# A state-space image block in float32: one norm stage's elementwise work spread over three engines, and an output stage that asks for its weights behind its first loads

## The chip, the cores and the metric

The kernel runs on one core of a Trainium2 chip. The core has five engines that the profile names: PE (matrix multiply, with its weight loads shown as PEld), DVE (vector), ACT (activation functions), POOL (general purpose) and SP, which here only issues DMAs. They run their own instruction streams and meet through semaphores. The metric is device time in microseconds (us) of one execution. All data is float32.

## The reference, cut to what matters

The input is an image `x` of 1024 channels by 64 x 64 pixels. Two blocks are computed, each added to its input:

```
x = x + conv(ln_c(x))            # ln_c: normalised over channels, at each pixel
t = tokens(x)                    # 4096 tokens (pixels) of 1024 channels
t = t + ffn(ln_t(t))             # ln_t: normalised over channels, at each token

conv(v):                         # a recurrence along the 1024 channels, for every pixel
    n  = layernorm2d(v) * w + b          # mean and variance over the 4096 pixels of a channel
    dt = softplus(n . dt_w + dt_b)       # n . dt_w sums over one image row of 64 pixels
    h[c] = exp(-exp(log_A) * dt[c]) * h[c-1] + n[c]      # out = h, for each pixel
ffn(v):
    x, z  = split(v @ in_proj)           # 2048 columns each
    y     = selective_scan(conv1d(x)) + the same backwards    # 16 states for each of 2048 columns
    out   = nan_to_num((y * silu(z)) @ out_proj)
```

The reference writes the recurrence of `conv` as a masked matrix of cumulative sums; it is the same function.

## The kernel before, in words

The program is six stages, one behind the other, each a block in which every engine has a written-out instruction list; a barrier stands between stages. Nothing is scheduled by a planner: the order on each engine is the order in the code, and loops (`Fori`) run on the engines with register addresses. A `wait_ge` holds an engine until a semaphore has reached a count; `then_inc` raises it when the instruction is done.

**Stages.** Channel norm, pixel variance, channel scan (`stage_channel_scan`, tensors `n_...` and `norm_...` in the trace), token norm, the large selective scan (`stage_scan`), and the output product (`stage_out`). The change touches the third and the last.

**Channel scan.** `xn`, the normalised input, stays in SBUF whole: 32 tiles of 128 pixels by 1024 channels. The loop takes two tiles (`s` = 0, 1) at a time, 16 pairs `j`. For a pair:

- POOL multiplies the tile by `rstd2` (L297, `scaled`). In the kernel before POOL waits for nothing here and goes through all 32 tiles at once, in place.
- DVE applies the affine part `* lnw + lnb`, in place (L315, `affine`, `normed`).
- PE sums image rows with the weights `dt_w` (L406, into PSUM `dt_ps`), and transposes the original input (L415, into PSUM `xt`).
- Softplus is `max(v, 0) + ln(1 + exp(-|v|))`: DVE does the maximum (L323, `relu`, reads PSUM), ACT does `Abs`, `Exp`, `Ln` (L384, L387, L390), DVE adds the two (L330, `add_log`, both inputs in SBUF).
- ACT forms the decay `exp(a * softplus)` (L395).
- DVE runs the recurrence (L336, `scan`: inputs `decay` and `xn`, both in SBUF), adds the transposed input (L341, one input in PSUM), takes statistics (L346, L350) and copies two numbers per tile (L353).

DVE's order inside the loop is `affine(j+1)`, `relu(j)`, `scan(j-1)`, `add_log(j)`. `relu(j)` waits for the decay of pair `j-1`, since both use the tile `softplus`.

**Output stage.** The 4096 tokens are 8 chunks of 512. For each chunk, 16 units of 128 columns are prepared: three loads of 256 KB (`yf`, `yb`, `z`), POOL adds `yb` to `yf` (L1278), ACT takes `silu(z)` (L1287), PE transposes the sum (L1299), DVE multiplies into `yg` (L1327). Then 8 projections follow (`project`, L1309): each is 16 matmuls of 512 columns that read all 16 units of `yg` and one eighth of the weights `wout` (1 MB), and DVE cleans, adds the residual and SP stores. `chunks` sets the order on every engine: chunk 0 is prepared whole, and from then on each step prepares one pair of units of the next chunk and then projects one eighth of this one. So PE transposes 18 units, the 16 of chunk 0 and the first pair of chunk 1, ahead of its first projection. SP runs one pair further ahead (`ahead=1`). The loads go into two buffers (`s`), reused when DVE has multiplied the unit (`gated`); the eight 1 MB loads of `wout` are asked for one at a time, one behind each pair of units of chunk 0 (L1256), and PE's first projection waits for all eight.

Of the kernel before, what the change touches and what calls it, by code (L numbers as in the profile page):

```python
# [260 lines left out]
def stage_channel_scan(nc, passed, xn, ident, rstd2, mv, x_d, lnw_d, lnb_d, dtw_d, dtb_d, loga_d):  # L261
    with Scope(nc, "n3") as sc:
# [30 lines left out]
        @block.gpsimd  # L293
        def _(pool):

            with pool.Fori(0, NT) as t:
                nc.gpsimd.tensor_tensor(xn[:, ds(t * C, C)], xn[:, ds(t * C, C)], rstd2[:],  # L297
                                        ALU.mult).then_inc(scaled, 1)

        @block.vector  # L300
        def _(dve):
# [10 lines left out]
            def affine(j):  # L312
                for s in range(2):
                    dve.wait_ge(scaled, j * 2 + s + 1)
                    nc.vector.tensor_scalar(xn[:, ds(j * (2 * C) + s * C, C)], xn[:, ds(j * (2 * C) + s * C, C)],  # L315
                                            lnw[:, ds(j * 2 + s, 1)], lnb[:, ds(j * 2 + s, 1)],
                                            ALU.mult, ALU.add).then_inc(normed, 1)

# [6 lines left out]

            def add_log(j):
                for s in range(2):
                    dve.wait_ge(log_done, j * 2 + s + 1)
                    dve.wait_ge(relu_done, j * 2 + s + 1)
                    nc.vector.tensor_tensor(sp_[:, s], sp_[:, s], mag[:, s], ALU.add).then_inc(sp_done, 1)  # L330
# [33 lines left out]
            affine(0)  # L364
            step(0, before=False)
            with dve.Fori(0, NT // 2 - 2) as i:
                step(i + 1)
            step(NT // 2 - 1, after=False)
# [3 lines left out]
        def _(act):  # L372
            act.wait_ge(par_loaded, 5 * LOAD)
            nc.scalar.activation(aneg[:], aneg[:], ACT.Exp).then_inc(achain, 1)
            act.wait_ge(achain, 1)
            nc.scalar.mul(aneg[:], aneg[:], -1.0).then_inc(achain, 1)
            act.wait_ge(achain, 2)
            act.sem_inc(decay_done, 2)
            act.sem_inc(scan_done, 2)
            with act.Fori(0, NT // 2) as j:  # L380
# [7 lines left out]
                for s in range(2):  # L388
                    act.wait_ge(ab_done, j * 4 + s + 3)
                    nc.scalar.activation(mag[:, s], mag[:, s], ACT.Ln, bias=1.0).then_inc(log_done, 1)  # L390
                for s in range(2):
                    act.wait_ge(par_loaded, 5 * LOAD)
                    act.wait_ge(sp_done, j * 2 + s + 1)
                    act.wait_ge(scan_done, j * 2 + s + 1)
                    nc.scalar.activation(decay[:, s], sp_[:, s], ACT.Exp,  # L395
                                         scale=aneg[:, ds(j * 2 + s, 1)]).then_inc(decay_done, 1)

# [800 lines left out]
def stage_out(nc, passed, ident, yf_d, yb_d, z_d, wout_d, x1T_d, out_d):  # L1198
    with Scope(nc, "out") as sc:
        wout = sc.sb("wout", [P, KT, DB, P])  # L1200
        yg = sc.sb("yg", [P, 2, DB, T])
        yf, yb = sc.sb("yf", [P, 2, T]), sc.sb("yb", [P, 2, T])
        z, sz = sc.sb("z", [P, 2, T]), sc.sb("sz", [P, 2, T])
# [4 lines left out]
        w_loaded, const_ready = sc.sem("w_loaded"), sc.sem("const_ready")  # L1208
        y_loaded, x_loaded = [sc.sem(f"y_loaded{s}") for s in range(2)], [sc.sem(f"x_loaded{s}") for s in range(2)]
# [7 lines left out]


# [23 lines left out]
        def _(sp):  # L1242
# [3 lines left out]
            def prepare(c, g, q):  # L1246
                for s in range(2):
                    db = 2 * q + s
                    hold(sp, gated, c * DB + db + 1, passed)
                    sp.dma_start(yf[:, s], yf_d[ds(c * DB + db + 1, 1)].rearrange("o p t d -> (o p) (t d)")  # L1250
                                 ).then_inc(y_loaded[s], LOAD)
                    sp.dma_start(yb[:, s], yb_d[ds((NCH - 1) * DB + db + 1 - c * DB, 1)]  # L1252
                                 .rearrange("o p t d -> (o p) (t d)")).then_inc(y_loaded[s], LOAD)
                    sp.dma_start(z[:, s], z_d[db * P:(db + 1) * P, ds(c * T, T)]).then_inc(y_loaded[s], LOAD)  # L1254
                if isinstance(c, int) and c == 0:
                    sp.dma_start(wout[:, q], wout_d[q]).then_inc(w_loaded, LOAD)  # L1256
# [13 lines left out]
        def _(pool):  # L1270
# [4 lines left out]
            def prepare(c, g, q):  # L1275
                for s in range(2):
                    pool.wait_ge(y_loaded[s], c * (KT * 3 * LOAD) + (q + 1) * 3 * LOAD)
                    nc.gpsimd.tensor_tensor(yf[:, s], yf[:, s], yb[:, s], ALU.add).then_inc(summed, 1)  # L1278
# [4 lines left out]
        def _(act):  # L1283
            def prepare(c, g, q):
                for s in range(2):
                    act.wait_ge(y_loaded[s], c * (KT * 3 * LOAD) + (q + 1) * 3 * LOAD)
                    nc.scalar.activation(sz[:, s], z[:, s], ACT.Silu).then_inc(silu_done, 1)  # L1287
# [4 lines left out]
        def _(pe):  # L1292
            def prepare(c, g, q):
                for s in range(2):
                    u = 2 * q + s
                    pe.wait_ge(summed, c * DB + u + 1)
                    pe.wait_ge(gated, c * DB + u + 1)
                    for tb in range(TB):
                        last = nc.tensor.matmul(yt_ps[:, s, tb * P:(tb + 1) * P], yf[:, s, tb * P:(tb + 1) * P],  # L1299
# [125 lines left out]
```

## Time and profile before

| | us |
|---|---|
| median of 3 runs | 8618.31 (8612.55 to 8621.57) |
| the profiled execution's own time | 8615.87 |
| its span, first to last instruction | 8614.1 |
| channel scan, 189.3 to 499.1 of the span | 309.8 |
| output stage, 7561.0 to 8614.1 | 1053.1 |
| of it, until the first projection starts at 7641.96 | 81.0 |

A row of the trace's timeline reads: start, duration, engine, line, operation, output <- inputs, shape, count; consecutive instructions of one line are merged, and the bracket says how long the engine sat idle before it and what ended that. A duration of merged instructions goes from the first start to the last end. A row of "windows" has the stretch and its length, then for PE, PEld, DVE, ACT and POOL the busy time and the number of instructions, then the granted clock of PE as a share of its full speed, the mean busy share of the 16 DMA engines and the rate in GB/s. A row of "waits" has who waited, for whom, us in total, times and the longest.

### The profile page before, as it was taken

What the parts mean: (1) busy time and instruction counts of PE and PEld (TensorE: products, weight loads), DVE (VectorE), ACT (ScalarE), POOL (GpSimd) and SP (SyncE); (2) the same over time, 40 slices, a digit from 0 to 9 for tenths busy, and PEclk for the clock granted to TensorE, in tenths of its full rate; (3) what the DMA queues carried; (4) which work ended last, traced back from release to release, by engine and by line L of the source; (5) the groups of instructions that cost most, each with busy time, mean ns of one, the idle gap of its engine ahead of it and who ended that gap; (6) DMA issues with size and microseconds to landing.
All of it is one profiled execution on the core that took longest, in us unless ns stands there. A gap on an engine that the chain in (4) does not pass through costs nothing. (4 is left out here: it accounts for less than half of the span.)

```text
span 8614.1 us, 107712 instructions
## 1 busy us (share of the span) xinstructions
PE 7207.2 (84%) x28624; PEld 4128.4 (48%) x28624; DVE 7548.3 (88%) x8364; ACT 4928.4 (57%) x11720; POOL 6814.0 (79%) x3026
## 2 busy tenths in 40 slices
PE   7449888888888888876788888888888887769999
PEld 4243455455545555544455545455555555534444
DVE  7940999999999999999999999999999999934443
ACT  2552666666666666666666666666666666610000
POOL 1310999999999999999999999999999999921110
PEclk9679999999999999987899999999999998879999
DMA  3263231313131313121223232323232322154442
GB/s 83 58 188 129 73 112 64 113 65 114 64 113 67 113 64 113 66 100 42 98 73 124 74 126 72 124 76 124 72 124 78 122 73 104 47 175 137 137 138 81
DMA packets 540787, 843.35 MB, mean 98 GB/s; under 512 B 112576, under 2 KB 260032, under 8 KB 522816
## 3 DMA queue, kind: packets, MB, share of 16 engines
q1 hardware_dynamic: 540224, 837.03, 29.4%
q8 instruction: 208, 3.41, 0.2%
q14 instruction: 355, 2.91, 0.1%
HBM read 583.83 MB, written 253.02 MB: 97 GB/s over the span
## 5 line engine op out<-in xcount | busy, mean ns | idle before, releaser
L1114 POOL TENSOR_TENSOR scan_w<-scan_du,scan_bcast_b 128x2048 f32<-128x2048 f32 x1023 | 4629.4, 4537 | 3.6 <-DMA scan_bcast_b<-bc 3.6
L1163 DVE TENSOR_TENSOR_SCAN scan_h<-scan_da,scan_state,scan_w 128x512 f32<-128x512 f32 x3072 | 3787.0, 1282 | 21.8 <-issue 14.5
L920 PE MATMUL scan_yT<-all_ident,scan_hc 128*128 128x128 f32 x12288 | 1992.4, 300 | 1010.9 <-DVE scan_hc L1173 995.5
L1020 ACT ACTIVATE scan_da<-scan_delta,scan_prm 128x512 f32<-128x512 f32 x4096 | 2803.6, 685 | 0.0
L920 PEld LDWEIGHTS scan_yT<-all_ident,scan_hc 128*128 128x128 f32 x12288 | 1466.6, 151 | 1974.6 <-DVE scan_hc L1173 1741.8
L1173 DVE TENSOR_TENSOR scan_hc<-scan_h,scan_bcast_c 128x512 f32<-128x512 f32 x3072 | 1955.5, 682 | 16.9 <-ACT scan_state L1000 16.9
L812 PE MATMUL scan_in_ps<-scan_hn,scan_win 128*128 128x512 f32 x3840 | 1741.0, 596 | 13.3 <-issue 13.3
L1000 ACT ACTIVATE scan_state<-scan_h 128x1 f32<-128x1 f32 x3072 | 518.6, 169 | 1770.7 <-DVE scan_h L1163 1768.8
L1123 POOL TENSOR_TENSOR scan_hp<-scan_hs,scan_bcast_c 128x512 f32<-128x512 f32 x1024 | 1306.5, 1276 | 73.7 <-issue 47.0
L1163 DVE TENSOR_TENSOR_SCAN scan_hs<-scan_da,scan_state,scan_w 128x512 f32<-128x512 f32 x1024 | 1297.5, 1267 | 32.1 <-ACT scan_da L1020 31.9
L812 PEld LDWEIGHTS scan_in_ps<-scan_hn,scan_win 128*128 128x128 f32 x3840 | 697.0, 192 | 723.2 <-issue 723.2
L1309 PE MATMUL out_o_ps<-out_yg,out_wout 128*128 128x512 f32 x2048 | 891.5, 594 | 0.0
L819 PE MATMUL scan_dt_ps<-scan_x,scan_diag 128*128 128x512 f32 x1920 | 882.3, 602 | 0.0
L1278 POOL TENSOR_TENSOR out_yf<-out_yf,out_yb 128x512 f32<-128x512 f32 x128 | 163.8, 1279 | 753.6 <-DMA out_z<-z 753.6
L887 PE MATMUL scan_yT<-all_ident,scan_hp 128*128 128x128 f32 x4096 | 714.3, 304 | 0.0
L1309 PEld LDWEIGHTS out_o_ps<-out_yg,out_wout 128*128 128x128 f32 x2048 | 386.1, 191 | 465.2 <-issue 465.2
L887 PEld LDWEIGHTS scan_yT<-all_ident,scan_hp 128*128 128x128 f32 x4096 | 562.4, 158 | 0.0
L1287 ACT ACTIVATE out_sz<-out_z 128x512 f32<-128x512 f32 x128 | 80.7, 630 | 836.2 <-DMA out_z<-z 836.2
L819 PEld LDWEIGHTS scan_dt_ps<-scan_x,scan_diag 128*128 128x128 f32 x1920 | 353.5, 194 | 356.9 <-issue 356.9
L1338 DVE COPY out_o<-out_o_ps 128x512 f32<-128x512 f32 x64 | 44.3, 692 | 523.4 <-PE out_o_ps L1309 316.5
L1000 ACT ACTIVATE scan_state<-scan_hs 128x1 f32<-128x1 f32 x1024 | 205.4, 201 | 318.2 <-DVE scan_hs L1163 317.1
L824 PE MATMUL scan_proj_ps<-scan_xc_out,scan_wx 128*96 128x512 f32 x512 | 384.1, 843 | 0.2
(128 smaller groups left out, 5547.8 us busy)
## 6 DMA issues: line engine op xcount, KB each, us to landing
yT<-scan_y_out SPq DMA_DIRECT2D x257, 256.0 KB, 2.0
scan_win<-winx SPq DMA_DIRECT2D x128, 512.0 KB, 3.5
xc<-scan_xc_out SPq DMA_DIRECT2D x256, 256.0 KB, 2.0
scan_xc<-xc SPq DMA_DIRECT2D x256, 256.0 KB, 3.6
scan_bcast_b<-bc SPq DMA_DIRECT2D x64, 1024.0 KB, 7.8
scan_bcast_c<-bc SPq DMA_DIRECT2D x64, 1024.0 KB, 7.8
scan_win<-winz SPq DMA_DIRECT2D x128, 512.0 KB, 4.6
scan_x<-x_pad SPq DMA_DIRECT2D x128, 257.5 KB, 2.6
```

What stands on the lines that cost most here:

```text
L812: last = nc.tensor.matmul(bank, win[:, s, i], hn[:, i], start=(i == 0), stop=(i == KT - 1))
L819: last = nc.tensor.matmul(bank, diag[:, s, i], x[:, s, at:at + T], start=(i == 0), stop=(i == TAPS - 1))
L824: nc.tensor.matmul(proj_ps[0:XO, :], wx[:, s], xc_out[:, s], start=False, stop=False).then_inc(S["proj_mm"], 1)
L887: last = nc.tensor.matmul(yT[:, tb], hp[:, i, tb * P:(tb + 1) * P], ident[:], is_transpose=True, start=False, stop=False)
L920: last = nc.tensor.matmul(yT[:, tb], hc[:, i % NOUT, tb * P:(tb + 1) * P], ident[:], is_transpose=True, start=(i == 0 and tb == 0), stop=( ...
L1000: nc.scalar.activation(state_of(unit_, n_), h_slot(n_)[:, col:col + 1], ACT.Copy).then_inc(S["h_saved"], 1)
L1020: nc.scalar.activation(da[:, n % 2], delta[:, s], ACT.Exp, scale=decay(b, n)).then_inc(S["exp_done"], 1)
L1114: nc.gpsimd.tensor_tensor(w[:, g], du[:, s].unsqueeze(1).to_broadcast([P, G, T]), bcast_b[:, g * G:(g + 1) * G], ALU.mult).then_inc(S["w_d ...
L1123: nc.gpsimd.tensor_tensor(hp[:, i], hs[:, i], bcast_c[:, n], ALU.mult).then_inc(S["hp_done"], 1)
L1163: nc.vector.tensor_tensor_scan(flip(b, h_slot(n)), flip(b, da[:, n % 2]), flip(b, w[:, n // G, n % G]), state_of(b, n), ALU.mult, ALU.add) ...
L1173: nc.vector.tensor_tensor(hc[:, i % NOUT], h_slot(n), bcast_c[:, n], ALU.mult).then_inc(S["hc_done"], 1)
L1309: last = nc.tensor.matmul(o_ps[:, q % 2], wout[:, q, b], yg[:, g, b], start=(b == 0), stop=(b == DB - 1))
```

## The change

In the channel scan, `affine` moves from DVE to ACT, as an `Identity` activation with scale and bias from `lnw` and `lnb`, and stands between `Ln` and the decay. `add_log` moves from DVE to POOL. POOL no longer scales all tiles at once: it scales two pairs, and then alternates `add_log(j)` and `scale(j+2)`. DVE's order becomes `relu(j+1)`, `scan(j)`. ACT loads one table set that holds `Exp` and `Ln` ahead of the loop. In the output stage the load buffers go from two to four, all of `wout` is asked for behind the last unit of chunk 0 with one semaphore for each eighth, and each projection waits for its own eighth.

```diff
@@ stage_channel_scan, POOL
-            with pool.Fori(0, NT) as t:
-                nc.gpsimd.tensor_tensor(xn[:, ds(t * C, C)], xn[:, ds(t * C, C)], rstd2[:],
-                                        ALU.mult).then_inc(scaled, 1)
+            def scale(j):
+                for s in range(2):
+                    nc.gpsimd.tensor_tensor(xn[:, ds(j * (2 * C) + s * C, C)], xn[:, ds(j * (2 * C) + s * C, C)],
+                                            rstd2[:], ALU.mult).then_inc(scaled, 1)
+            def add_log(j):
+                for s in range(2):
+                    pool.wait_ge(relu_done, j * 2 + s + 1)
+                    pool.wait_ge(log_done, j * 2 + s + 1)
+                    nc.gpsimd.tensor_tensor(sp_[:, s], sp_[:, s], mag[:, s], ALU.add).then_inc(sp_done, 1)
+            scale(0)
+            scale(1)
+            with pool.Fori(0, NT // 2 - 2) as j:
+                add_log(j)
+                scale(j + 2)
+            add_log(NT // 2 - 2)
+            add_log(NT // 2 - 1)
@@ DVE (affine and add_log taken out)
-            def step(j, before=True, after=True):
-                if after:
-                    affine(j + 1)
-                relu(j)
-                if before:
-                    scan(j - 1)
-                add_log(j)
...
+            relu(0)
+            with dve.Fori(0, NT // 2 - 1) as i:
+                relu(i + 1)
+                scan(i)
+            scan(NT // 2 - 1)
@@ ACT (abs, exp, ln as before)
+            def affine(j):
+                for s in range(2):
+                    act.wait_ge(scaled, j * 2 + s + 1)
+                    nc.scalar.activation(xn[:, ds(j * (2 * C) + s * C, C)], xn[:, ds(j * (2 * C) + s * C, C)],
+                                         ACT.Identity, bias=lnb[:, ds(j * 2 + s, 1)],
+                                         scale=lnw[:, ds(j * 2 + s, 1)]).then_inc(normed, 1)
...
+                if after:
+                    affine(j + 1)
...
+            nc.scalar.preload_act_table_set("natural_log_exp_and_others")
@@ stage_out
-        yf, yb = sc.sb("yf", [P, 2, T]), sc.sb("yb", [P, 2, T])
-        z, sz = sc.sb("z", [P, 2, T]), sc.sb("sz", [P, 2, T])
+        NY = 4
+        yf, yb = sc.sb("yf", [P, NY, T]), sc.sb("yb", [P, NY, T])
+        z, sz = sc.sb("z", [P, NY, T]), sc.sb("sz", [P, NY, T])
...
+        def slot(q, s):
+            return q % 2 * 2 + s
...
-                if isinstance(c, int) and c == 0:
-                    sp.dma_start(wout[:, q], wout_d[q]).then_inc(w_loaded, LOAD)
+                if isinstance(c, int) and c == 0 and q == KT - 1:
+                    for i in range(KT):
+                        sp.dma_start(wout[:, i], wout_d[i]).then_inc(w_loaded[i], LOAD)
...
             def project(c, g, q):
+                pe.wait_ge(w_loaded[q], LOAD)
                 if q == 0:
-                    pe.wait_ge(w_loaded, KT * LOAD)
-                    pe.wait_ge(gated, c * DB + DB + 2)
+                    pe.wait_ge(gated, c * DB + DB + NY)
...
-            dve.sem_inc(gated, 2)
+            dve.sem_inc(gated, NY)
```

PE's transposes still wait for the unit two before to be multiplied (two PSUM buffers, as before).

ACT's loop of the channel scan before (`n_mag` is the softplus logarithm in the making, `n_decay` the decay):

```order
L384 ACTIVATE n_mag<-n_dt_ps,n_dtb 128x1024
...
L387 ACTIVATE n_mag<-n_mag 128x1024
...
L390 ACT_TABLE_LOAD
L390 ACTIVATE n_mag<-n_mag 128x1024
...
L395 ACT_TABLE_LOAD
L395 ACTIVATE n_decay<-n_softplus,n_aneg 128x1024
```

And after:

```order
L376 ACTIVATE n_mag<-n_dt_ps,n_dtb 128x1024
...
L379 ACTIVATE n_mag<-n_mag 128x1024
...
L382 ACTIVATE n_mag<-n_mag 128x1024
...
L368 ACTIVATE norm_xn<-norm_xn,n_lnb,n_lnw 128x1024
...
L388 ACTIVATE n_decay<-n_softplus,n_aneg 128x1024
```

Two table loads leave the loop, and the affine activation stands ahead of the decay. POOL's list of the same stage, before:

```order
L296 ISA
L297 ISA
L297 TENSOR_TENSOR norm_xn<-norm_xn,norm_rstd 128x1024
L296 REGISTER_ALU
L296 COMPARE_AND_BRANCH
```

And after (four scalings stand ahead of the loop):

```order
L298 TENSOR_TENSOR norm_xn<-norm_xn,norm_rstd 128x1024 x4
L309 UNCONDITIONAL_BRANCH
L309 ISA
L305 TENSOR_TENSOR n_softplus<-n_softplus,n_mag 128x1024
L303 REGISTER_ALU
L305 TENSOR_TENSOR n_softplus<-n_softplus,n_mag 128x1024
L298 ISA
L298 TENSOR_TENSOR norm_xn<-norm_xn,norm_rstd 128x1024
L298 ISA
L298 TENSOR_TENSOR norm_xn<-norm_xn,norm_rstd 128x1024
```

POOL's work in a loop turn is now two additions and then two scalings. SP's list at the end of chunk 0's units in the output stage, before:

```order
L1250 DMA out_yf<-yT 128x512
L1252 DMA out_yb<-yT 128x512
L1254 DMA out_z<-z 128x512
L1256 DMA out_wout<-wout 128x2048
```

And after:

```order
L1263 DMA out_yf<-yT 128x512
L1265 DMA out_yb<-yT 128x512
L1267 DMA out_z<-z 128x512
L1270 DMA out_wout<-wout 128x2048 x8
L1263 DMA out_yf<-yT 128x512
L1265 DMA out_yb<-yT 128x512
L1267 DMA out_z<-z 128x512
```

The eight weight loads stand together behind unit 15 of chunk 0, and ahead of the first two units of chunk 1.

## Rows read from the trace of the kernel before

**Rows 1.** Windows: channel scan; output stage until its first projection
```profile
189.00:500.00 311.00, 129.50 (x384) 69.11 (x384) 295.32 (x292) 176.18 (x164) 92.24 (x33) 0.67 0.20 54
7561.00:7642.00 81.00, 19.91 (x73) 13.11 (x74) 11.76 (x17) 12.62 (x19) 24.20 (x21) 0.50 0.82 282
```

**Rows 2.** Timeline of DVE, one turn of the loop with POOL idle
```profile
344.84 2.48 DVE L323 TENSOR_SCALAR n_softplus<-n_dt_ps,n_dtb 128x1024 f32<-128x1024 f32 x2
347.23 4.46 DVE L336 TENSOR_TENSOR_SCAN n_scanned<-n_decay,norm_xn 128x1024 f32<-128x1024 f32 x2
351.61 2.33 DVE L341 TENSOR_TENSOR norm_xn<-n_scanned,n_xt 128x1024 f32 x2
357.00 2.36 DVE L330 TENSOR_TENSOR n_softplus<-n_softplus,n_mag 128x1024 f32<-128x1024 f32 x2
360.93 2.48 DVE L323 TENSOR_SCALAR n_softplus<-n_dt_ps,n_dtb 128x1024 f32<-128x1024 f32 x2
```

**Rows 3.** Timeline of DVE, the loop while POOL scales, and its last turn
```profile
194.18 11.17 DVE L315 TENSOR_SCALAR norm_xn<-norm_xn,n_lnw,n_lnb 128x1024 f32<-128x1024 f32 x4
224.53 2.46 DVE L323 TENSOR_SCALAR n_softplus<-n_dt_ps,n_dtb 128x1024 f32<-128x1024 f32 x2
226.92 8.73 DVE L336 TENSOR_TENSOR_SCAN n_scanned<-n_decay,norm_xn 128x1024 f32<-128x1024 f32 x2
240.63 2.03 DVE L353 COPY norm_mv<-n_mv_t 128x2 f32 x2
252.50 2.47 DVE L323 TENSOR_SCALAR n_softplus<-n_dt_ps,n_dtb 128x1024 f32<-128x1024 f32 x2
473.56 2.48 DVE L323 TENSOR_SCALAR n_softplus<-n_dt_ps,n_dtb 128x1024 f32<-128x1024 f32 x2 [1.56 <-ACT n_decay L395]
```

**Rows 4.** POOL's scaling: one line's durations (min/median/max ns), and two stretches of timeline
```profile
L297 POOL TENSOR_TENSOR norm_xn<-norm_xn,norm_rstd x32: 2332/2709/4272, 189.5 to 280.1; 128x1024 f32 x32
226.85 6.65 POOL L297 TENSOR_TENSOR norm_xn<-norm_xn,norm_rstd 128x1024 f32 x2
242.61 3.39 POOL L297 TENSOR_TENSOR norm_xn<-norm_xn,norm_rstd 128x1024 f32 x1
```

**Rows 5.** The page's costliest groups: POOL and DVE in the large scan
```profile
L1114 POOL TENSOR_TENSOR scan_w<-scan_du,scan_bcast_b 128x2048 f32<-128x2048 f32 x1023 | 4629.4, 4537 | 3.6 <-DMA scan_bcast_b<-bc 3.6
L1163 DVE TENSOR_TENSOR_SCAN scan_h<-scan_da,scan_state,scan_w 128x512 f32<-128x512 f32 x3072 | 3787.0, 1282 | 21.8 <-issue 14.5
```

**Rows 6.** Timeline of ACT and PE, the same turn as rows 2; and ACT in the token norm
```profile
347.41 5.86 PE L406 MATMUL n_dt_ps<-norm_xn,n_row_w 128*128 x8 [8.42 <-ACT n_mag L384]
348.36 1.99 ACT L387 ACTIVATE n_mag<-n_mag 128x1024 f32<-128x1024 f32 x2
351.66 2.00 ACT L390 ACTIVATE n_mag<-n_mag 128x1024 f32<-128x1024 f32 x2
502.63 2.37 ACT L481 ACTIVATE n_hn<-norm_xn,n_nmr,n_rstd 128x1024 f32 x2 [0.99 <-DVE n_nmr L464]
```

**Rows 7.** DMA packets in two stretches of one microsecond, from 7569 and from 7572
```profile
DMA packets 54, 0.43 MB, mean 434 GB/s; under 512 B 1, under 2 KB 1, under 8 KB 1
DMA packets 202, 0.35 MB, mean 350 GB/s; under 512 B 31, under 2 KB 31, under 8 KB 202
```

**Rows 8.** Timeline of the output stage: first load, last unit's addition, first two projections
```profile
7561.26 0.34 SPq L1250 DMA_DIRECT2D out_yf<-yT  x1
...
7639.74 1.26 POOL L1278 TENSOR_TENSOR out_yf<-out_yf,out_yb 128x512 f32<-128x512 f32 x1 [2.10 <-DMA out_z<-z]
7641.96 15.94 PE L1309 MATMUL out_o_ps<-out_yg,out_wout 128*128 128x512 f32 x32
7658.62 13.90 PE L1309 MATMUL out_o_ps<-out_yg,out_wout 128*128 128x512 f32 x32
```

**Rows 9.** Waits of PE and of SP, 7642 to 8481
```profile
PE out_yt_ps L1299 <- POOL out_yf L1278: 23.0, 28, 2.2
SPq L47 <- DVE out_yg L1327: 2.6, 7, 1.6
```

More of the change, by code:

```diff
@@ L310, in _ @@
             dve.sem_inc(added, 2)
[L312 to L317, printed above, removed]
             def relu(j):
@@ L324, in relu @@
                                             ALU.max).then_inc(relu_done, 1)
[L326 to L330, printed above, removed]
             def scan(j):
@@ L372, in _, with step @@
         def _(act):
[L373 to L380, printed above, removed]
+            def affine(j):
[4 more added lines that the diff above has]
+                                         scale=lnw[:, ds(j * 2 + s, 1)]).then_inc(normed, 1)
+            def step(j, after=True):
                 for s in range(2):
@@ L396, in _ @@
                                          scale=aneg[:, ds(j * 2 + s, 1)]).then_inc(decay_done, 1)
+            nc.scalar.preload_act_table_set("natural_log_exp_and_others")
+            act.wait_ge(par_loaded, 5 * LOAD)
+            affine(0)
+            nc.scalar.activation(aneg[:], aneg[:], ACT.Exp).then_inc(achain, 1)
+            act.wait_ge(achain, 1)
+            nc.scalar.mul(aneg[:], aneg[:], -1.0).then_inc(achain, 1)
+            act.wait_ge(achain, 2)
+            act.sem_inc(decay_done, 2)
+            act.sem_inc(scan_done, 2)
+            with act.Fori(0, NT // 2 - 1) as j:
+                step(j)
+            step(NT // 2 - 1, after=False)
         @block.tensor
@@ L1207, in stage_out @@
         yt_ps, o_ps = sc.ps("yt_ps", [P, 2, T]), sc.ps("o_ps", [P, 2, T])
-        w_loaded, const_ready = sc.sem("w_loaded"), sc.sem("const_ready")
-        y_loaded, x_loaded = [sc.sem(f"y_loaded{s}") for s in range(2)], [sc.sem(f"x_loaded{s}") for s in range(2)]
+        w_loaded, const_ready = [sc.sem(f"w_loaded{q}") for q in range(KT)], sc.sem("const_ready")
+        y_loaded, x_loaded = [sc.sem(f"y_loaded{s}") for s in range(NY)], [sc.sem(f"x_loaded{s}") for s in range(2)]
         o_stored = [sc.sem(f"o_stored{s}") for s in range(2)]
@@ L1285, in prepare @@
                 for s in range(2):
-                    act.wait_ge(y_loaded[s], c * (KT * 3 * LOAD) + (q + 1) * 3 * LOAD)
-                    nc.scalar.activation(sz[:, s], z[:, s], ACT.Silu).then_inc(silu_done, 1)
+                    i = slot(q, s)
+                    act.wait_ge(y_loaded[i], y_loads(c, q))
+                    nc.scalar.activation(sz[:, i], z[:, i], ACT.Silu).then_inc(silu_done, 1)
             chunks(act, prepare, lambda c, g, q: None)
@@ L1296, in prepare @@
                     pe.wait_ge(summed, c * DB + u + 1)
-                    pe.wait_ge(gated, c * DB + u + 1)
+                    pe.wait_ge(gated, c * DB + u + NY - 1)
                     for tb in range(TB):
-                        last = nc.tensor.matmul(yt_ps[:, s, tb * P:(tb + 1) * P], yf[:, s, tb * P:(tb + 1) * P],
+                        last = nc.tensor.matmul(yt_ps[:, s, tb * P:(tb + 1) * P], yf[:, slot(q, s), tb * P:(tb + 1) * P],
                                                 ident[:], is_transpose=True, start=(tb == 0), stop=(tb == TB - 1))
```

27 lines of the change are left out of this document (12 added, 15 removed).

## The prediction, made before the changed kernel ran

> **What bounds the kernel now.** I first read the windows. The channel scan is held by DVE, busy 295 of 311 us [rows 1]. The output stage until its first projection is held by the DMA engines: 0.82 busy with every compute engine idle most of the time [rows 1]. Everything between the two stages and after them has the same instructions in both kernels, so I count it as unchanged.
>
> In the channel scan the timeline of DVE shows two regimes. With POOL idle a turn (two tiles) takes 16.09 us, 344.84 to 360.93 [rows 2], and DVE has no gap. While POOL scales, a turn takes 28.0, 224.53 to 252.50 [rows 3]. The extra 12 us are in instructions that read two SBUF tensors, or are short copies: two scans take 8.73 instead of 4.46, two copies 2.03, while the maximum with its PSUM input stays at 2.47 [rows 2, 3]. POOL's scaling takes 2.33 at best and 4.27 at worst [rows 4]. Both engines lose about what the other one uses: POOL's two operations from 226.85 end at 233.50, the first in about 2.4, the second in 4.27, which is 2.33 behind one scan of 2.2. So I read it as one at a time: whoever asks first runs, the other waits for the end. Two copies in 2.03 say more: DVE waits for POOL's operation once and then gets both short copies through before POOL's next one has started. Worked forward over the whole stage with this rule, these durations give slow turns of 28 to 30 us and an end near 499, which is where the stage ends.
>
> **The channel scan, step by step.** DVE loses `add_log` and `affine`, 357.00 to 360.93, 3.93 us per turn [rows 2]. It keeps 12.16. ACT gets two affine activations; the nearest row is a scale-and-bias activation of the same size, 2.37 for two [rows 6]. It loses both table loads (ACT's list in the section on the change). Its turn is about 2.2 + 2.0 + 2.0 + 2.4 + 2.2 = 10.8, inside DVE's. POOL now has four operations of 2.33 in each turn, 9.3. No engine is over 12.2 by itself; what sets the turn is the ring through all of them. I count from the start of the first maximum:
>
> - `Exp` starts 3.52 later, 344.84 to 348.36 [rows 2, 6]. Two `Exp` 2.0, first `Ln` 1.0: at 6.5.
> - POOL then does addition, addition, scaling: 3 x 2.33 = 7.0, at 13.55.
> - DVE arrives at its two copies at about 11.8 (12.16 less the copies), while the first scaling runs. They wait 1.75 for its end, pass both (0.35), and the next maximum starts at 13.95.
>
> The second scaling runs beside the maxima, which read PSUM and don't wait (2.39 us against 2.33). The scans start as it ends, and POOL then waits for `Ln`, so scans and POOL miss each other by a few tenths. The turn is 14.0.
>
> The other ring goes through PE: at 7.5 both `Ln` are done, first affine 1.2, then the matmuls of both tiles, 5.86 for eight [rows 6]: 14.6 for the second tile, whose maximum stands 1.2 behind the first, so 13.4. That ring is shorter, if PE's clock stays as it is. At the lower of its two levels (1.2 GHz) throughout, eight would take 8 x 2 x 13.90/32 = 6.95 [rows 8], and the ring 14.5.
>
> Start and end: before, four affines ran beside POOL from 194.18 for 11.17 us, and the first maximum came at 205.3 [rows 3]. Now ACT does two at 1.2 each, PE needs some 3.4 for the first tile, so the first maximum comes near 198.5. Fifteen turns at 13.9 on average (the last has no scaling in its way) give 207.5, the last maximum at 406. Behind it DVE has two turns' work less one pair of maxima, 21.9, and about 1 of waiting: 429. Before it was 473.56 [rows 3] and 499.1. The term is -70. Of it, some 33 come from the first three turns, which were slow, 25 from 2.1 us on twelve others, and the rest from the two ends.
>
> What hides ACT's new work is its own idle time ahead of the decay; the decay is wanted only after POOL's addition. The affine delays the decay of the first tile until 9.9, and POOL's addition ends at 8.9: 1 us, not on the ring.
>
> **A rule of the skill against the trace.** In the large scan DVE's recurrence of 512 columns takes 1282 ns beside a POOL that is busy nearly throughout with operations of 4537 ns that read SBUF [rows 5]; half of a 1024-column scan is 1.1 to 1.2. Nothing waits there. The Trainium skill, page "SBUF — State Buffer", section "Who interferes with whom", has it that a DVE instruction with two SBUF inputs and a GpSimd one that reads SBUF block each other for the whole instruction. Rows 3 and 4 agree with that, rows 5 don't, and I don't know what differs. By the rule the turn is 14.0; by rows 5 it is the third case below.
>
> **The output stage until its first projection.** PE's list has 18 units ahead of the first projection, 16 of chunk 0 and two of chunk 1, and SP now asks for all 8 MB of weights ahead of those last two. The packets show that the queue serves in order: in the microsecond from 7569 nearly all packets are of the 8 KB kind (weights), from 7572 all are of the small kind [rows 7]: the weights are through before the unit asked for behind them starts. So the weights don't get out of the way; they only move from between the units to ahead of the last two. The first projection needs the same 18 x 0.786 + 8 x 1.049 = 22.5 MB as before. What can be gained is the 18% in which the DMA engines are idle, since four units are in flight instead of two. From below: 22.84 MB took 0.82 x 81 = 66.4 us of busy engines, so 22.5 MB at full share take 65.5. To it come 1.5 for the first issue and 2.2 from the last landing to the projection (7639.74 to 7641.96 [rows 8]): 69.2 against 80.7 since the first issue at 7561.26 [rows 8], a gain of 11.5. From above, at the rates of rows 7 (0.35 and 0.434 MB/us): 40.4 + 19.3 + 3.7 = 63.4, a gain of 17. I take -12, nearer to the first, since the small packets' rate in one good microsecond isn't that of sixty; the ends are -4 (the pacing stays imperfect) and -17.
>
> **The projections.** Four buffers let SP ask for a unit without waiting for `gated`, but before each pair SP still stands behind the store of the last projection, in its own order. Of waits on `gated` the queue shows 2.6 us in all, and PE waits 23.0 us for POOL's sums, 28 times [rows 9]. Loads that start 0.1 us earlier at 28 of those give 3. I take -3, between 0 and -8. The new wait of PE in each projection is on weights that land 2.4 us apart while a projection takes 13.9 [rows 8]: nothing waits.
>
> **Sum.** 8615.87 - 70 - 12 - 3 = 8530.9 by the profiled execution. The median of the runs is 2.4 above it, so 8533.
>
> **Rivals.**
> 1. Copies go through one at a time. If POOL's next operation gets in between the two copies, each waits for a whole one: the ring becomes 16.4, 14 turns cost 2.4 more, +34: 8567. Two in 2.03 speaks against it [rows 3], but POOL's two scalings follow each other with a different start each time.
> 2. Slower: POOL's operations meet DVE's scans too. Place: the second scaling is still running when the scan asks, DVE slips, and every one of the four POOL operations is waited for in turn. The turn is then 12.2 + 9.3 = 21.5, the stage ends at 198.5 + 15 x 21.5 + 23 = 544, +45 - 15: 8648. It decides from a turn of 19.5, where the stage's loss eats the output's gain. The slow turns of rows 3 show such a pile-up (12 us in 28); against it, POOL there never waited for anything, and now it waits for `Ln` just while the scans run.
> 3. Nothing waits for POOL, as in rows 5. The turn is the ring through PE, about 13.2: -11, 8522. With PE at the lower level throughout it is 14.5, and 8541.
> 4. The order of the queue isn't kept, and the last two units pass the weights. Then the first projection needs 14.2 MB and one eighth: another -20, 8513. Rows 7 speak against it.
> 5. The change does less than it says: the activation costs more on ACT than its neighbour's row, or the loads stay paced as now. With 2 us more per turn and no gain at the output: 8533 + 28 + 12 = 8573.
>
> **Chances.** The forecast, 14.0 per turn and output gains near 15, has 0.52, with an own range of 8522 to 8546. Rival 1 has 0.14, rival 2 0.04, rival 3 0.14, rival 4 0.05, rival 5 0.11. Below 8512 or above 8575 I leave about 0.14. Differences under 0.2% (17 us) can't be told from none in this kernel. Faster than that: 0.94; within: 0.02; slower: 0.04.
>
> **What would show it.** The scan stage should end near 429, DVE's turns be 14.0 with the only long wait inside the copies (about 2.1 for two), scans at 4.4 for two, and ACT without table loads in the loop. If scans take more than 5 for two, rival 2's mechanism is there. The first projection should start 12 us earlier than 81.0 into its stage, and the eight weight packets' stretch should lie between unit 15 and unit 16. The forecast fails if DVE's turn isn't between 13.2 and 14.6.

## The result, and the profile after

The changed kernel took 8528.89 us (median of 4 runs, 8523.32 to 8533.4), the kernel before 8615.43 beside it (8612.47 to 8621.57). The ratio is 0.9898, with an interval of 0.9881 to 0.9915: 86.5 us saved. The forecast was 8533. The profiled execution of after is its fastest, 8523.32; its span is 8521.3, which is 92.8 below the profiled one of before. By stage, from the two traces:

| | before | after | difference | forecast |
|---|---|---|---|---|
| end of the channel scan, at | 499.03 | 427.69 | -71.3 | -70 |
| from there to the first load of the output stage | 7062.2 | 7056.7 | -5.5 | 0 |
| from that load to the first projection | 80.7 | 66.4 | -14.3 | -12 |
| from the first projection to the end | 972.1 | 970.5 | -1.6 | -3 |

The windows of after, same columns as [rows 1] (length; busy of PE, PEld, DVE, ACT, POOL; granted clock; DMA share; GB/s). The first is the channel scan, the second the output stage until its first projection:

```profile
189.00:435.00 246.00, 129.70 (x403) 71.56 (x404) 219.98 (x232) 173.07 (x168) 152.99 (x68) 0.72 0.26 69
7484.40:7551.00 66.60, 20.08 (x73) 13.30 (x74) 11.75 (x17) 12.96 (x20) 24.53 (x22) 0.50 0.98 363
```

DVE's busy time fell from 295 to 220 us and POOL's rose from 92 to 153. In the output stage the DMA engines went from 0.82 busy to 0.98: almost nothing of the stretch is idle time of theirs.

DVE's timeline, one turn of the loop and the start of the next:

```profile
268.82 2.66 DVE L331 TENSOR_SCALAR n_softplus<-n_dt_ps,n_dtb 128x1024 f32<-128x1024 f32 x2
271.39 4.46 DVE L338 TENSOR_TENSOR_SCAN n_scanned<-n_decay,norm_xn 128x1024 f32<-128x1024 f32 x2
280.84 1.90 DVE L355 COPY norm_mv<-n_mv_t 128x2 f32 x2
282.65 2.57 DVE L331 TENSOR_SCALAR n_softplus<-n_dt_ps,n_dtb 128x1024 f32<-128x1024 f32 x2
```

The turn is 13.83 where [rows 2] had 16.09 and [rows 3] 28.0. The scans take 4.46, as [rows 2] had them; in [rows 3], beside POOL, they took 8.73. They don't meet POOL any more: it waits for `Ln` while they run. The two copies take 1.90, though alone they need 0.38 (at 417.56, where POOL has no work left). What they wait for stands in POOL's and ACT's timelines:

```profile
280.30 4.66 POOL L298 TENSOR_TENSOR norm_xn<-norm_xn,norm_rstd 128x1024 f32 x2
289.36 4.71 POOL L305 TENSOR_TENSOR n_softplus<-n_softplus,n_mag 128x1024 f32<-128x1024 f32 x2 [4.40 <-ACT n_mag L382]
```

```profile
288.16 1.99 ACT L382 ACTIVATE n_mag<-n_mag 128x1024 f32<-128x1024 f32 x2
290.06 2.36 ACT L368 ACTIVATE norm_xn<-norm_xn,n_lnb,n_lnw  x2
```

The first scaling runs from 280.30 for about 2.33. The copies come at 280.84, stand until it ends, and the next maximum starts at 282.65. The second scaling lies beside the maxima, and POOL then waits 4.40 for `Ln` while DVE scans. There is no table load between the activations.

One turn went differently. From 225.26 to 241.16 it took 15.9, and the copies were the reason:

```profile
237.08 4.17 DVE L355 COPY norm_mv<-n_mv_t 128x2 f32 x2
```

Two waits of a POOL operation each, in place of one: that is rival 1's mechanism, once in the fifteen turns of this execution. The ten turns from 254.79 take 14.03 down to 13.65, on average 13.73. In these turns a second ring, the one through PE, closes at the same moment. In one of the last of them PE's sums for the second tile end at 352.26, and that tile's maximum starts 0.04 behind them:

```profile
346.23 6.03 PE L412 MATMUL n_dt_ps<-norm_xn,n_row_w 128*128 x8 [5.88 <-ACT norm_xn L368]
```

```profile
352.30 1.28 DVE L331 TENSOR_SCALAR n_softplus<-n_dt_ps,n_dtb 128x1024 f32<-128x1024 f32 x1
```

The output stage, SP's issues (start, duration, and the number of DMAs in the group):

```profile
7484.39 0.34 SPq L1263 DMA_DIRECT2D out_yf<-yT  x1
...
7519.52 4.58 SPq L1270 DMA_DIRECT2D out_wout<-wout  x8
...
7529.40 6.21 SPq L1267 DMA_DIRECT2D out_z<-z  x1
```

And POOL's sum of unit 16 (that of unit 15 ran at 7524.53, for 1.26), with PE's first projection behind it:

```profile
7546.44 1.26 POOL L1293 TENSOR_TENSOR out_yf<-out_yf,out_yb 128x512 f32<-128x512 f32 x1 [20.65 <-DMA out_z<-z]
```

```profile
7550.78 15.04 PE L1325 MATMUL out_o_ps<-out_yg,out_wout 128*128 128x512 f32 x32
```

The 20.65 us between unit 15 and unit 16 are the eight weight loads, as the order of the queue demands.

### The profile page after: what moved, and what is told of

It reads as the page before. It is cut to its first block and busy times, and to the rows that moved or that the text cites. A ratio compares the mean times of both kernels' runs of the same rounds, so it can differ in the third digit from the quotient of the medians.

```text
span 8521.3 us, 107499 instructions
## 1 busy us (share of the span) xinstructions
PE 7199.0 (84%) x28624; PEld 4125.5 (48%) x28624; DVE 7468.1 (88%) x8300; ACT 4922.4 (58%) x11720; POOL 6869.8 (81%) x3058
## 5 line engine op out<-in xcount | busy, mean ns | idle before, releaser
L1179 DVE TENSOR_TENSOR scan_hc<-scan_h,scan_bcast_c 128x512 f32<-128x512 f32 x3072 | 1935.4, 669 | 16.3 <-ACT scan_state L1006 16.3
L1303 ACT ACTIVATE out_sz<-out_z 128x512 f32<-128x512 f32 x128 | 80.7, 630 | 820.6 <-DMA out_z<-z 820.6
```

The source lines that it names most:

```text
L1179: nc.vector.tensor_tensor(hc[:, i % NOUT], h_slot(n), bcast_c[:, n], ALU.mult).then_inc(S["hc_done"], 1)
```

## Experiments

The times stand beside runs of the kernel before on the same chip: 8611.8 (25 runs) for the first four, 8612.79 (9) for the next three.

**scan_only.** The changed channel scan, the output stage as before:

```diff
@@ the kernel before, with the changed stage_channel_scan
-            with pool.Fori(0, NT) as t:
-                nc.gpsimd.tensor_tensor(xn[:, ds(t * C, C)], xn[:, ds(t * C, C)], rstd2[:],
+            with pool.Fori(0, NT // 2 - 2) as j:
+                add_log(j)
+                scale(j + 2)
```

> Only the channel scan is changed, the output stage is as before. If the two parts are independent and the stage times of the profile are right (scan stage 71.3 us shorter, output 14.3 and 1.6), it is 70 to 73 us faster than before, near 8544, and the scan stage ends at 428 of the span. Rival: the stretch between the two stages, 5.5 us shorter in the changed kernel's profile though its instructions are the same, depends on the channel scan; then it is 76 to 78 faster. If those 5.5 us are spread between executions, the stretch comes out anywhere between 7056 and 7063.

8544.9 us, ratio 0.9924 (0.9907 to 0.994): -66.9. The stage ended at 424.49, 3.2 earlier than in after: no copies waited twice here, and the settled turn was 13.64. From the first load to the first projection it was 80.75, as before. This trace has POOL's ring alone. PE's sums end at 335.44, and the maximum that needs them starts only 0.20 later, because DVE comes late from its copies:

```profile
329.58 5.86 PE L412 MATMUL n_dt_ps<-norm_xn,n_row_w 128*128 x8 [6.05 <-ACT norm_xn L368]
```

```profile
335.64 1.27 DVE L331 TENSOR_SCALAR n_softplus<-n_dt_ps,n_dtb 128x1024 f32<-128x1024 f32 x1
```

The stretch between the stages took 7056.4, so the 5.5 us that it differs between before and after don't come from either part of the change: over all runs it is 7056.4 to 7062.4, whatever the kernel.

**out_only.** The other half alone:

```diff
@@ the kernel before, with the changed stage_out
-        yf, yb = sc.sb("yf", [P, 2, T]), sc.sb("yb", [P, 2, T])
+        NY = 4
+        yf, yb = sc.sb("yf", [P, NY, T]), sc.sb("yb", [P, NY, T])
```

> Only the output stage is changed. Expected 14 to 16 us faster than before, near 8600, with the first projection 66.4 us behind the first load (80.7 before). The rival that the middle stretch depends on the output part gives 20 to 22.

8594.17 us, ratio 0.9981 (0.9971 to 0.999): -17.6. First load to first projection: 65.0. With scan_only that makes -84.5, against -86.5 for both: the parts add up, as far as intervals of some 8 and 14 us to each side can say.

**out_four.** out_only with the weights back at their old places:

```diff
-                if isinstance(c, int) and c == 0 and q == KT - 1:
-                    for i in range(KT):
-                        sp.dma_start(wout[:, i], wout_d[i]).then_inc(w_loaded[i], LOAD)
+                if isinstance(c, int) and c == 0:
+                    sp.dma_start(wout[:, q], wout_d[q]).then_inc(w_loaded[q], LOAD)
```

> The kernel before with four load buffers in the output stage, weights still asked for between the pairs of units. The DMA queue serves in order and the first projection needs the same 22.5 MB either way, so by my theory the whole 14.3 us come from the buffers: the first projection starts 66 to 67 us behind the first load. Rival: grouping the weights behind unit 15 is worth something by itself (fewer switches between small and large packets); then this kernel starts its first projection 3 us or more later than out_only.

8591.9 us, ratio 0.9977 (0.9968 to 0.9987): -19.9.

**out_order.** out_only with two buffers:

```diff
-        NY = 4
+        NY = 2
...
-            return q % 2 * 2 + s
+            return s
```

> The kernel before with two load buffers, but all weights asked for behind unit 15 of chunk 0, and one semaphore each. By my theory this is a loss: with two units in flight the weights between the units were what kept the DMA engines busy while a buffer came free. Sixteen units at about 5 us apart in pairs of 6.5 to 7.5 us give 52 to 60 us, then 8.4 MB and two units in 24 to 26: first projection 80 to 92 us behind the first load, kernel 0 to 12 us slower than before. Rival: the order is what gives the 14 us; then the first projection comes at 66 to 70.

8621.9 us, ratio 1.0011 (1.0001 to 1.002): +10.1. The windows from the first load to the first projection, out_four first, then out_order:

```profile
7556.80:7619.60 62.80, 19.88 (x73) 13.09 (x73) 11.76 (x17) 12.84 (x20) 24.40 (x22) 0.50 1.01 381
```

```profile
7559.00:7650.00 91.00, 19.89 (x73) 13.09 (x74) 11.76 (x17) 12.54 (x19) 24.11 (x21) 0.50 0.71 248
```

The whole gain of this part comes from the buffers. With two of them, a weight load behind each pair kept the queue working while SP stood for the next free buffer (share 0.82 in [rows 1]); with the weights taken away from there nothing does, the share is 0.71, and 10 us are lost. With four buffers the block of weights seems to cost 2 to 4 us: 65.0, 66.4 and 66.9 in the three traces that have it against 62.7 here, a difference that the medians don't separate.

**affine_only.** The kernel before with only the affine on ACT, and the table set loaded once. DVE keeps the addition, POOL scales all tiles at once:

```diff
@@ DVE
-            def affine(j):
...
+            relu(0)
+            add_log(0)
+            with dve.Fori(0, NT // 2 - 1) as i:
+                relu(i + 1)
+                scan(i)
+                add_log(i + 1)
@@ ACT: affine(j + 1) behind Ln, natural_log_exp_and_others ahead of the loop, as in the change
```

> The kernel before with one part of the channel scan's change: the affine step on ACT with one table set. POOL still scales all tiles at once, DVE still adds the logarithm, output stage as before. Theory (one at a time): beside POOL's scaling a turn is still slow, about 24 us for three turns (28.0 less the affine's share), then DVE's own 14.5; the stage ends near 466, 33 us earlier than before. So the two other parts (addition on POOL, scaling paced by it) would be worth the remaining 38. Rival: the slow turns come from the affine step meeting POOL; then three turns of about 16 and an end near 442, 57 earlier.

8582.94 us, ratio 0.9965 (0.9953 to 0.9978): -29.9. The stage ended at 468.4. A turn with POOL idle took 14.77, one beside POOL 22.5, with two additions at 4.50 and two scans at 8.45; DVE there:

```profile
235.10 8.45 DVE L329 TENSOR_TENSOR_SCAN n_scanned<-n_decay,norm_xn 128x1024 f32<-128x1024 f32 x2
```

The rival that wanted an end near 442 falls. Scans and additions still lose POOL's time beside a POOL that never stops. So of the stage's 71 us some 31 come with the affine and the table loads, and 41 need the addition on POOL together with POOL's work spread over the turns.

**act_copy.** The changed kernel with its last long wait removed: the two short copies go to ACT, two turns late, between `Abs` and `Exp`:

```diff
-                for s in range(2):
-                    dve.wait_ge(chain, j * 6 + s + 3)
-                    nc.vector.tensor_copy(mv[:, ds(j * 4 + s * 2, 2)], mv_t[:, s]).then_inc(chain, 1)
+            def move(p):
+                for s in range(2):
+                    act.wait_ge(chain, p * 4 + s + 3)
+                    nc.scalar.activation(mv[:, ds(p * 4 + s * 2, 2)], mv_t[:, s], ACT.Identity).then_inc(moved, 1)
```

> The changed kernel with the two short copies of each turn moved from DVE to ACT, everything else as it is. Theory: the copies are the place where DVE waits for POOL's first scaling (1.90 for two, 0.38 without a wait); without them the turn falls from 13.7 to 13.8 to the next ring, 13.2 to 13.5 through PE, or the scans now meet the second scaling by a few tenths: turn 13.2 to 13.6, stage end 421 to 425 in place of 427.7, kernel 3 to 7 us faster than the changed one. Rival A: the wait moves whole to the scans, since POOL's second scaling is then still running: turn as before, 13.7 to 14, scans over 5 for two. Rival B: the copies' wait isn't on the ring at all; then the turn stays at 13.7 with an idle DVE ahead of the maximum.

8520.83 us, ratio 0.9895 (0.9878 to 0.9911). A gain of 3 to 7 us over after (0.9898) is too small for these intervals, so the trace has to decide. The stage ended at 425.76, against 427.69 in after, where one turn had lost 2.1, and at 424.49 in scan_only, which still has the copies on DVE. The turn settles at 13.65, from 14.21 at the start. So nothing was gained, and DVE now stands in front of the maxima:

```profile
280.38 1.28 DVE L331 TENSOR_SCALAR n_softplus<-n_dt_ps,n_dtb 128x1024 f32<-128x1024 f32 x1 [0.95 <-ACT n_decay L393]
282.47 1.28 DVE L331 TENSOR_SCALAR n_softplus<-n_dt_ps,n_dtb 128x1024 f32<-128x1024 f32 x1 [0.80 <-PE n_dt_ps L422]
```

```profile
276.57 5.86 PE L422 MATMUL n_dt_ps<-norm_xn,n_row_w 128*128 x8 [6.07 <-ACT norm_xn L366]
```

Both waits are for PE. The first maximum needs the first tile's sums, the first four of these eight matmuls, which end at 280.35; the second needs the other four, to 282.43. The view puts the first wait down to a decay that ended at 280.36, but the one that the program asks for there is the first tile's, done at 278.50. This is what rival B expected: the turn as it was, with an idle DVE in front of the maximum. The theory's 13.2 to 13.6 is missed, if by little. And the experiment made PE's ring longer itself: on ACT the two copies stand between `Abs` and `Exp` and hold `Exp` back by 0.19. Without them that ring would be near 13.5.

**spread_act_copy.** act_copy, and PE is let start on the first eighths: three of them are asked for behind the first two units of chunk 1, one more in each of the first five projections' steps (chunks 0 and 1 are written out ahead of the loop for it):

```diff
-                if isinstance(c, int) and c == 0 and q == KT - 1:
-                    for i in range(KT):
+                if isinstance(c, int) and c == 1 and q == 0:
+                    for i in range(3):
...
+                if isinstance(c, int) and c == 0 and q + 3 < KT:
+                    sp.dma_start(wout[:, q + 3], wout_d[q + 3]).then_inc(w_loaded[q + 3], LOAD)
```

> act_copy, and in the output stage the weights asked for in another order: three eighths behind the first two units of chunk 1, one more in each of the first five projection steps; chunks 0 and 1 are written out ahead of the loop for that. Theory (the queue serves in order, the first projection needs what stands ahead of it): the first projection needs 18 units and one eighth, 15.2 MB in place of 22.5, so it starts 43 to 47 us behind the first load (66.4 in the changed kernel), and the later eighths land while projections run, which use a third of the queue's rate: 18 to 22 us faster than act_copy, near 8503. Rival: loads of the next units now stand behind an eighth each and come late, PE waits 1 to 3 us in each of the first steps; then 8 to 14 faster.

8491.72 us, ratio 0.986 (0.9843 to 0.9876): -121, and 29.1 under act_copy, more than expected. It is the fastest version. First load to first projection fell from 66.9 to 46.1, which is the part that was expected. The stretch behind it took 966.7 against 970.4, but that one is 966.0 to 975.1 in kernels that have before's output stage, so these traces don't say where the other 8 us are. PE's first projections:

```profile
7529.24 16.54 PE L1340 MATMUL out_o_ps<-out_yg,out_wout 128*128 128x512 f32 x32
7546.49 13.90 PE L1340 MATMUL out_o_ps<-out_yg,out_wout 128*128 128x512 f32 x32
```

No wait for weights stands between them. The first is the slower one in every run (15.04 to 16.54, here at a granted clock of 0.84); the second takes 13.90 while the other eighths land, as everywhere. The stretch was full of transfers, so what shortened it was to take transfers out of it, and the semaphore for each eighth, which the change already has, allows that.

The next five ask why DVE and POOL exclude each other in the channel scan and not in [rows 5]. All are single executions, the kernel before beside them at 8614.83 (first three) and 8606.36.

**b_scratch2.** The kernel before, POOL's scaling written elsewhere (what follows works on unscaled data):

```diff
-                nc.gpsimd.tensor_tensor(xn[:, ds(t * C, C)], xn[:, ds(t * C, C)], rstd2[:],
-                                        ALU.mult).then_inc(scaled, 1)
+                    pool.wait_ge(scaled, j * 2 + s + 1)
+                    nc.gpsimd.tensor_tensor(scr[:, s], xn[:, ds(j * (2 * C) + (2 + s) * C, C)], rstd2[:],
+                                            ALU.mult).then_inc(scaled, 1)
```

> The kernel before with POOL's scaling written to two scratch tiles in place of back into xn; what follows works on unscaled data, the other instructions and their order are the same. In the large scan POOL's operations write to another tile than they read, and DVE doesn't wait for them; in the channel scan and in the output stage they work in place, and DVE waits. If working in place is what makes the two engines exclude each other, the slow turns of 28.0 vanish: turns of 16.1 from the start, scans 4.46 for two. If it's enough that both read two SBUF tensors, nothing changes: 8.7 for two scans, turns of 28.

8649.41 us, +34.6. Neither expectation came true. DVE's first instruction behind POOL's start, which is short, and POOL beside it:

```profile
193.13 69.93 DVE L314 TENSOR_SCALAR n_row_w<-n_row_w,n_dtw 128x128 f32<-128x128 f32 x1 [3.26 <-DMA n_dtb<-dt_b]
193.94 69.04 POOL L302 TENSOR_TENSOR n_scr<-norm_xn,norm_rstd 128x1024 f32<-128x1024 f32 x30
```

DVE stood for all of POOL's 30 operations, one behind the other, and went on as the last ended.

**b_state.** The kernel before, the scan started from a column in SBUF, as the large scan's is:

```diff
-                    nc.vector.tensor_tensor_scan(scanned[:, s], decay[:, s], xn[:, ds(j * (2 * C) + s * C, C)], 0.0,
+                    nc.vector.tensor_tensor_scan(scanned[:, s], decay[:, s], xn[:, ds(j * (2 * C) + s * C, C)], dtb[:],
```

> The kernel before with the channel scan's recurrence started from a column in SBUF (the bias dtb, so the result differs by that start value) in place of the constant 0, the form that the large scan uses. If that form is what doesn't wait for POOL, two scans take 4.5 beside POOL and a turn of the slow stretch about 23.8. If not, 8.7 and 28.

8609.8 us, scans 8.73, turn 27.96: this form isn't what differs.

**b_copy.** The kernel before, POOL with a copy of one input in place of the multiplication:

```diff
-                nc.gpsimd.tensor_tensor(xn[:, ds(t * C, C)], xn[:, ds(t * C, C)], rstd2[:],
-                                        ALU.mult).then_inc(scaled, 1)
+                nc.gpsimd.tensor_copy(xn[:, ds(t * C, C)], xn[:, ds(t * C, C)]).then_inc(scaled, 1)
```

> The kernel before with POOL's scaling replaced by a copy in place (one SBUF input, the scaling is left out). A POOL copy of this size takes 1.04 us. If the exclusion holds for any POOL instruction that reads SBUF, scans still wait: two scans 4.5 plus up to two copies of 1.0, that is 5.5 to 6.5, for as long as POOL runs (32 copies, 33 us and what it waits). If only POOL's two-input form excludes, scans take 4.5 and copies 0.38 throughout.

8576.03 us. The copies take 1.04 each on POOL (the median of 32). Two scans of DVE beside them:

```profile
216.86 5.67 DVE L335 TENSOR_TENSOR_SCAN n_scanned<-n_decay,norm_xn 128x1024 f32<-128x1024 f32 x2
```

A one-input operation makes DVE wait too, for its own shorter time: 5.67 - 4.46 = 1.2 for two scans. By the Trainium skill, page "SBUF — State Buffer", section "Who interferes with whom", it is enough that the GpSimd instruction reads SBUF for a DVE one with two SBUF inputs to meet it; the trace agrees.

**a_scratch, a_place.** To see what DVE's two-input instructions do, both start from affine_only and let POOL begin behind DVE's preparations (`pool.wait_ge(setup, 4)`). a_scratch writes elsewhere, a_place is the same program in place:

```diff
@@ a_place against a_scratch
-                    nc.gpsimd.tensor_tensor(scr[:, s], xn[:, ds(j * (2 * C) + (2 + s) * C, C)], rstd2[:],
+                    nc.gpsimd.tensor_tensor(xn[:, ds(j * (2 * C) + (2 + s) * C, C)], xn[:, ds(j * (2 * C) + (2 + s) * C, C)], rstd2[:],
```

> affine_only with POOL's scaling of all 32 tiles written to two scratch tiles (what follows works on unscaled data), begun only when DVE's setup is done. In b_scratch2 DVE's first instruction beside such a POOL, a tensor_scalar with one SBUF input, waited 69.9 us, to POOL's last operation. Here the first that meets POOL is the addition of two SBUF tensors, the kind that in the large scan never waits. Theory 1 (POOL's operations, 2.44 long and begun every 2.30, hand the shared port to each other, and any DVE instruction that needs it waits for the last): the first addition waits until POOL ends at about 267, some 60 us, and all turns behind it are 14.6. Theory 2 (two-input instructions don't need the port against a POOL that writes elsewhere, as in the large scan; only one-input copies and tensor_scalar do): additions 2.36 and scans 4.46 for two beside POOL, and the first pair of short copies waits for POOL's end.

> The same program as a_scratch, its wait in POOL's loop too, but the scaling is in place, and so complete. Theory 1 leaves open what lets DVE in: if it's the place (in place gives DVE a gap), DVE's turns are 22.5 beside POOL, as in affine_only, and POOL's operations begin 2.33 or more apart. If it was the wait in POOL's loop that closed the gap in b_scratch2, the first addition waits for POOL's last operation here as well.

8614.45 and 8587.41 us, +8.1 and -19.0. DVE in a_scratch, and in a_place:

```profile
207.11 61.85 DVE L329 TENSOR_TENSOR n_softplus<-n_softplus,n_mag 128x1024 f32<-128x1024 f32 x2 [4.02 <-ACT n_mag L381]
```

```profile
240.65 8.38 DVE L334 TENSOR_TENSOR_SCAN n_scanned<-n_decay,norm_xn 128x1024 f32<-128x1024 f32 x2
...
255.82 6.66 DVE L328 TENSOR_TENSOR n_softplus<-n_softplus,n_mag 128x1024 f32<-128x1024 f32 x2
```

Theory 1 came true: the first addition waited for POOL's last operation. The two programs differ in the place that POOL writes to and in nothing else, so in this stage it is the place, not the wait in POOL's loop. In place DVE gets its turn behind each operation; elsewhere it gets none until the last. The turn of a_place was 24.4, not the 22.5 that was expected: two additions took 6.66, where affine_only had 4.50. Why they lose more here isn't known.

## Why the prediction was right

**The mechanism of the turn.** It was that DVE and POOL run one at a time, and that the new order leaves one meeting per turn, in the copies. The trace has it so: the copies 1.90 (about 2.1 forecast), the scans 4.46 and unhindered, the second scaling beside the maxima. The turn was forecast at 14.0; it settles at 13.65 in after and 13.64 in scan_only. Three turns lie outside 13.2 to 14.6: the first (13.12), the last (12.60, with no scaling in its way) and the one of 15.90. affine_only and a_place confirm the rule for POOL's work in place. The 0.35 between 14.0 and 13.65 is the term for passing both copies. The first copy ends with POOL's scaling, and the second and the next maximum follow at once: in a settled turn the scaling ends at 351.09 and the maximum starts at 351.10.

**The channel scan's ends.** First maximum 198.5 forecast, 197.70 measured; last 406 against 404.66; end 429 against 427.69. The working has a slip here: fifteen turns at 13.9 are 208.5, not 207.5. That the end came within 1.3 us is partly luck. The turns were shorter than thought, the one with the copies' second wait gave 2.1 back, and those behind it began at up to 14.03. scan_only, which has neither, ended at 424.49: -74.5 by its trace, where -70 was forecast.

**The ring through PE** was sized about right: 13.4 in the working, and in scan_only PE is ready 0.18 to 0.30 before the maximum in turns of 13.64. What the working left open was PE's clock, and it moved the ring. The eight matmuls took 5.86 in scan_only at a granted clock of 0.63, between the levels of 1.2 and 2.4 GHz. In after they took 6.39 at 0.57 at the end of the long turn, in which PE had stood idle for 8.35 us, later 6.03 at 0.61 behind 5.88 of idle time, and with that the ring was 13.65, as long as POOL's. The two rings differ so little that the copies' wait was worth no more than some 0.2 per turn. For rival 3 it matters: it counted 13.2, which the working doesn't give; with no meeting at all and 13.4 per turn its gain over the forecast would have been about 8 us, not 11.

**The output prologue.** Forecast -12 by bytes over a full queue, measured -14.3. The DMA engines were busy 0.98 of 66.6, 65.3 us, where the working had 65.5 for the bytes at full share. That these agree is partly luck: 363 GB/s over 66.6 us are 24.2 MB, more than the 22.5 that the first projection needs, since other transfers ran beside the first issue and the last landing. Per busy microsecond after moved 0.370 MB, before only 0.344 (282 GB/s at 0.82). At after's rate the 22.5 MB need 61 us, and 5.5 go to the two ends, for which the working had 3.7. So the rate was taken too low (by 4.6 us) and the ends too short (by 1.8): the working counted 69.2 in all and 66.4 came out. That this part moves by its buffers and not by the order was said in the working, and out_four and out_order show it: -19.9 and +10.1. The rival in which the last two units pass the weights falls with POOL's 20.65 us.

**The projections.** -3 forecast, -1.6 measured, and neither is shown: from the first projection to the end, kernels with before's output stage took 966.0 to 975.1. The first projection went from 15.94 [rows 8] to 15.04, but that is the granted clock (0.87, then 0.92), and it was 16.46 in scan_only and 15.25 in out_only. PE's waits for POOL's sums behind it stayed as they were, here from the waits of after, 7551 to the end (us in total, times, longest), against 23.0 [rows 9]:

```profile
PE out_yt_ps L1315 <- POOL out_yf L1293: 22.7, 28, 2.5
```

So the term's reason, loads that start earlier at 28 places, was wrong: the waits fell by 0.3, not 3. Only its size was small enough not to matter.

**The sum.** -85 forecast; -86.5 by the medians, -92.8 by the spans. The spans compare two single executions, and that of after is the fastest of its four, 5.6 under their median, that of before 0.4 over its own. By stage, 5.5 of the 92.8 lie in the stretch that the change doesn't touch and whose length goes from 7056.4 to 7062.4 between executions. Without them -87.3 are left.

**Open.** Why in the large scan DVE never waits beside POOL [rows 5] isn't settled. Its POOL operation writes elsewhere, and is nearly back to back; by a_scratch it should stop DVE altogether. b_state took away one difference. Others (block length, 2048 columns, a broadcast operand) weren't tried.

## What to carry to other kernels

Draw each ring through all engines before cutting one: when the copies' wait was taken away, the ring through PE stood 0.2 us behind it, the new copies on ACT used that up, and nothing was gained. Where a stretch is short of overlap, more buffers fill it (0.82 to 0.98); where it is full, moving bytes behind the first consumer's need shortens it (66.9 to 46.1). A long unbroken list on POOL beside a DVE that reads SBUF can be dear (turns of 28.0 in the channel scan) or cost nothing ([rows 5]), so look at DVE's durations beside it. Where it is dear, give POOL its work in pieces, with a wait in each turn at the point where DVE has its instructions with two SBUF inputs.

## What the hardware showed that I had not expected

- POOL's back-to-back multiplications that write to another tile kept DVE out for 69.93 and 61.85 us, for one instruction and for two. The Trainium skill, page "SBUF — State Buffer", section "Who interferes with whom", has it that whoever issues first holds the shared ports for the whole instruction and the other is blocked. That describes the work in place, but not a wait over thirty instructions. In place, the same operations let DVE in between any two of them, at one wait each (two scans 8.38 to 8.73 instead of 4.46). The two that write to another tile are single executions.
- An issue on SP isn't always short: with the weights outstanding, the one of `z` at 7529.40 took 6.21 us, where others took 0.34. The trace shows no cost of it: the loads behind it stood in the same full queue.
